# Flamingo-style gated cross attention with routed experts, one core: queries from column-major input and centred weights, the root moved to maxima and exponentials, attention order rewritten

## The reference

```python
x = x + tanh(g_xattn[0]) * xattn(layernorm(x), ctx, Wq, Wkv, null_kv, Wout, ln_scale, ln_bias)
x = x + tanh(g_ffn[0]) * ffn(layernorm(x), ...)      # 32 routed experts, top 8, and a shared one

# xattn
q = split_heads(x @ Wq) * DH ** -0.5
k, v = split_heads(context @ Wkv)                     # null_kv is put in front
attn = softmax(q @ k.T)                               # over 78 columns
out = (attn @ v) @ Wout
out = (out - mean(out)) * rsqrt(var(out) + 1e-6) * ln_scale + ln_bias
```

## Time and profile before

| | us |
|---|---|
| three runs | 2053.12, 2056.40, 2056.99 |
| median | 2056.4 |
| the profiled execution | 2052.15 |
| its span in the trace | 2050.1 |

### The profile page before, as it was taken

The page is one execution under the profiler, slowest core; times in us unless marked ns, Lnnn a source line. Parts: engine busy times, 40 slices in busy tenths (PEclk is TensorE's granted clock), DMA queues, the critical chain, the costliest instruction groups (busy, mean ns, idle before and its releaser), DMA issues.

```text
span 2050.1 us, 43651 instructions
## 1 busy us (share of the span) xinstructions
PE 1947.4 (95%) x14658; PEld 1735.4 (85%) x14658; DVE 1623.5 (79%) x3801; ACT 1377.7 (67%) x3988; POOL 1156.9 (56%) x1254
## 2 busy tenths in 40 slices
PE   7999799999999999999977899999999999999995
PEld 7998689999999999899866788888888888888884
DVE  5544248888888888888867666679999999999996
ACT  2100078888888888888853477777777777777761
POOL 0000103777777777777776000047777777777775
PEclk9999899999999999999978999999999999999997
DMA  8543388877777777777768999999999999999998
GB/s 268 170 143 132 108 307 307 293 253 246 252 250 255 254 247 246 248 255 252 249 229 295 373 285 288 286 327 402 403 393 397 390 398 393 391 397 396 387 363 285
DMA packets 319571, 605.45 MB, mean 295 GB/s; under 512 B 87510, under 2 KB 191671, under 8 KB 319351
## 3 DMA queue, kind: packets, MB, share of 16 engines
q1 hardware_dynamic: 270198, 468.39, 65.7%
q0 software_dynamic: 49152, 134.28, 18.0%
HBM read 305.00 MB, written 297.53 MB: 294 GB/s over the span
## 4 chain that ended last, share of the span: by engine, by line
PE 50%; DMA 17%; DVE 13%; issue 3%; ACT 3%; SPq 2%; DVEq 0%; ACTq 0%
DMA w_raw<-in_experts 15%; PE ring L140 6%; PE sim L1262 6%; PE ring L1326 6%; PE ring L1309 6%; PE ring L141 6%; PE ring L142 6%; DVE parts L1805 4%; PE xps L1902 2%; DVE up_ps L1856 2%; DVE hid_l L1862 2%; DVE w_l L1779 2%; PE gate_ps L140 1%; DVE wq_l L1767 1%; PE gate_ps L141 1%
## 5 line engine op out<-in xcount | busy, mean ns | idle before, releaser
L1696 POOL DMA_INDIRECT parts<-results_dram,kept_index x512 | 516.5, 1009 | 387.2 <-DMA results_dram<-y 219.4
L789 POOL DMA_INDIRECT pages_dram<-rows,kept_index x512 | 537.6, 1050 | 156.2 <-issue 150.0
L847 ACT ACTIVATE exps<-sim,minus_max 128x78 f32<-128x78 f32 x1024 | 317.3, 342 | 23.4 <-DVE minus_max L964 22.6
L1717 ACT ACTIVATE w_h<-w_raw 128x768 fp32r<-128x768 f32 x159 | 134.1, 843 | 157.9 <-DMA w_raw<-in_experts 157.9
L847 ACT ACTIVATION_READ_ACCUMULATOR exps<-sim,minus_max 128x1 f32 x1024 | 229.1, 224 | 0.0
L1805 DVE SCALAR_TENSOR_TENSOR parts<-parts,kept_weight 128x256 f32<-128x256 f32 x448 | 214.0, 478 | 1.3 <-DMA parts<-dense_dram 0.2
L1902 PE MATMUL xps<-ident,xin 128*128 128x128 f32 x1272 | 167.2, 275 | 20.2 <-DVE wq_l L1767 11.5
L1779 DVE TENSOR_TENSOR w_l<-w_raw,w_h 128x768 fp32r<-128x768 f32 x159 | 151.7, 954 | 43.2 <-ACT w_h L1717 42.9
L140 PE MATMUL yps<-w_h,hid_h 128*128 128x256 f32 x636 | 179.5, 282 | 1.4 <-DVE hid_l L1862 1.3
L142 PE MATMUL yps<-w_l,hid_h 128*128 128x256 f32 x636 | 178.4, 281 | 0.0
L141 PE MATMUL yps<-w_h,hid_l 128*128 128x256 f32 x636 | 178.1, 280 | 0.0
(11 more groups left out here) (239 smaller groups left out, 5930.8 us busy)
## 6 DMA issues: line engine op xcount, KB each, us to landing
xin<-pages_dram SPq DMA_DIRECT2D x159, 512.0 KB, 10.5
results_dram<-y SPq DMA_DIRECT2D x159, 512.0 KB, 9.6
w_raw<-in_experts SPq DMA_DIRECT2D x159, 385.0 KB, 9.4
pages_dram<-blank SPq DMA_DIRECT2D x108, 512.0 KB, 4.2
pages_dram<-blank SPq DMA_DIRECT2D x12, 1536.0 KB, 7.0
keys_dram<-keys SPq DMA_DIRECT2D x16, 616.0 KB, 4.3
kT<-keys_dram SPq DMA_DIRECT2D x32, 308.0 KB
v<-values_dram SPq DMA_DIRECT2D x32, 308.0 KB
```

Of the source, the lines that this page charges most:

```text
L789: pool.indirect_dma_start(dram["pages"], bass.IndirectOffsetOnAxis(ap=kept_index[:, at:at + 1].bitcast(U32), axis=0), buffer(batch)[:, k / ...
L847: last = act.activation(exps[u % 2][:, h, :], scores(u)[:, h % 2, h // 2, :], ACT.Exp, bias=minus_max[u][:, h:h + 1], accum_out=row_sum[u] ...
L1696: pool.indirect_dma_start(parts[slot(batch, t)][:, k, :], None, done, bass.IndirectOffsetOnAxis(ap=kept_index[:, at:at + 1].bitcast(U32), ...
```

## The change

- **Queries.** The mean of a row is taken out by centring the columns of Wq instead of the row of x: in the context stage PE multiplies a constant matrix (1/8 by 1/256) with Wq into two free PSUM banks (four products of 512 columns), and DVE subtracts that from Wq/8 in place (four passes of 128x512) before the split. x comes a second time as an input laid out by columns (`in_x_cols`), which is loaded straight into two buffers in turn and split into high and low from SBUF. `apply_x`, the transposes of X and its place in the ring are gone.
- **The root.** The queries lack the factor rstd of their token. DVE multiplies the negated maxima of a unit by it (`scale_maximum`, 128x8, after `maximum`, with a semaphore between), and the exponential takes it as its scale column.
- **Order.** RING, BANK, COPIED and the steps of PE, ACT, DVE, SP and GpSimd are written anew: T1 stands before L and similarity 3, PV0 before the Qs, Q0 to Q2 together, T2b after T3; one scatter moves from between the roots to behind the second; on DVE both parts of `normalise` 0 and 1 come earlier and `weigh` later.

```diff
-RING = ["Oa", "X", "N2", "Ob", "T0a", "T0b", "L", "Q0", "T1a", "Q1", "T1b", "R", "Q2", "PV0a", "PV0b", "T2a", "T2b", "T3a",
-        "T3b", "Q3", "PV1a", "PV1b"]
+RING = ["Oa", "N2", "Ob", "T0a", "T0b", "T1a", "T1b", "L", "PV0a", "PV0b", "Q0", "Q1", "Q2", "T2a", "R", "T3a", "T3b",
+        "T2b", "Q3", "PV1a", "PV1b"]
+BANK = {"Oa": 3, "N2": 2, "Ob": 3, "T0a": 0, "T0b": 1, "T1a": 2, "T1b": 0, "L": 1, "PV0a": 2, "PV0b": 0, "Q0": 1, "Q1": 3,
+        "Q2": 2, "T2a": 1, "R": 3, "T3a": 0, "T3b": 2, "T2b": 1, "Q3": 3, "PV1a": 0, "PV1b": 3}
+COPIED = ["N2", "T0a", "T0b", "X", "T1b", "T1a", "PV0a", "PV0b", "Q0", "Q1", "Q2", "T2a", "T3a", "T2b", "T3b", "Q3", "PV1a",
...
 # context stage, DVE
+            for i in QUERY:
+                dve.wait_ge(averaged, 2)
+                for h in range(INNER // 512):
+                    cols = slice(h * 512, (h + 1) * 512)
+                    last = dve.scalar_tensor_tensor(out=staged(i)[:, cols], in0=staged(i)[:, cols], scalar=SCALE, in1=mean_bank(h)[:, :],
+                                                    op0=ALU.mult, op1=ALU.subtract)
+                last.then_inc(centred, 1)
 # context stage, PE, after the second group's products
+                    for h in range(INNER // 512):
+                        pe.wait_ge(lo, at(CRING, PRODUCTS[len(PRODUCTS) - CBANK + h], g))
+                        for i in QUERY:
+                            pe.wait_ge(w_loaded[i % STAGES], 16 * (i // STAGES + 1))
+                            last = pe.matmul(mean_bank(h)[:, :], column_means[:, :], staged(i)[:, h * 512:(h + 1) * 512],
+                                             start=i == QUERY[0], stop=i == QUERY[-1])
 # attention, SP
-                sp.wait_ge(applied[0], b + 2)
-                sp.dma_start(x_in[:, :, :], x_tiles[b + 2]).then_inc(x_loaded, 16)
+                if b >= 0:
+                    sp.wait_ge(ring_lo, nth(SPLIT, "X", b - 1))
+                load_x(b + 2)
 # GpSimd
-                scatter(b, range(2, 10))
+                scatter(b, range(2, 9))
 # ACT
                 last = act.activation(exps[u % 2][:, h, :], scores(u)[:, h % 2, h // 2, :], ACT.Exp,
-                                      bias=minus_max[u][:, h:h + 1], accum_out=row_sum[u][:, h:h + 1])
+                                      bias=minus_max[u][:, h:h + 1], scale=norm["rstd"][:, b * TT + u % 2:b * TT + u % 2 + 1],
+                                      accum_out=row_sum[u][:, h:h + 1])
-            high("Q0", b)
-            high("T1a", b)
+            high("PV0a", b)
             if here:
                 exp(3, b, 0, PAIRS // 2)
-            high("Q1", b)
-            high("T1b", b)
+            high("PV0b", b)
             if here:
                 exp(3, b, PAIRS // 2, PAIRS)
+            high("Q0", b)
+            high("Q1", b)
             high("Q2", b)
...
 # DVE
-                              ALU.max, negate=True).then_inc(max_done, 1)
+                              ALU.max, negate=True).then_inc(max_made, 1)
+        def scale_maximum(u, b):
+            dve.wait_ge(max_made, UNITS * b + u + 1)
+            dve.tensor_scalar(minus_max[u][:, :], minus_max[u][:, :], norm["rstd"][:, b * TT + u % 2:b * TT + u % 2 + 1], None,
+                              ALU.mult).then_inc(max_done, 1)
 # PE
-            if name == "X":
-                pe.wait_ge(applied[0], b + 2)
-                for c in range(DC):
-                    for t in range(TT):
-                        last = pe.transpose(ps[:, c * N + t * P:c * N + (t + 1) * P], xn[:, t, c * P:(c + 1) * P], ident[:, :])
-                pe.wait_ge(ring_hi, nth(COPIED, ("T1b", "T3a")[half], b))
+                pe.wait_ge(ring_hi, nth(COPIED, ("T1a", "T3b")[half], b))
```

More of the change, by code:

```diff
@@ L214, in context_phase @@
               for j in range(0, 2 * INNER, COLS)]
-    pieces += [(dram["Wq"][c * P:(c + 1) * P, :], [w[:, c, :] for w in wq], SCALE) for c in range(DC)]
+    pieces += [(dram["Wq"][c * P:(c + 1) * P, :], [w[:, c, :] for w in wq], 1.0) for c in range(DC)]
     of_piece = PIECE // D
@@ L566, in attention_phase @@
     grown = sb("grown", [P, ROUTED])
-    x_in = sb("x_in", [P, TT, D])
-    xn = sb("xn", [P, TT, D])
+    x_cols = [sb(f"x_cols{i}", [P, DC, N]) for i in range(2)]
     xnT = [sb(f"xnT_{s}", [P, DC, N], F32R) for s in "hl"]
@@ L583, in attention_phase @@
     gate_ready, rows_ready = sem("gate_ready"), sem("rows_ready")
-    x_loaded, res_loaded = sem("x_loaded"), sem("res_loaded")
+    x_loaded, res_loaded = [sem(f"x_loaded{i}") for i in range(2)], sem("res_loaded")
     keys_loaded = sem("keys_loaded")
@@ L810, in step @@
             if scatters:
-                scatter(b, range(10, 16))
+                scatter(b, range(9, 16))
             if b == B:
@@ L876, in apply_rows @@
             last.then_inc(applied[2], 1)
[L878 to L881, removed]
-                act.wait_ge(norm["ready"], 1)
-            for t in range(TT):
-                at = batch * TT + t
-                last = act.activation(xn[:, t, :], x_in[:, t, :] if batch else rows[0][:, t, 0:D], ACT.Identity,
-                                      bias=norm["shift"][:, at:at + 1], scale=norm["rstd"][:, at:at + 1])
-            last.then_inc(applied[0], 1)
         def step(b, par, h):
@@ L940, in step @@
                 next(dense)
+            high("PV1b", b)
             if 1 <= b <= B:
@@ L1159, in step @@
                 sum_weights(b - 4)
+            if here:
+                scale_maximum(1, b)
             if b >= 3:
@@ L1169, in step @@
                 next(dense)
-            if b >= 3:
-                match(b - 3)
-            if b >= 3:
-                scale_weights(b - 3)
-            if b >= -1:
-                low("X", b)
-            if 1 <= b <= B:
-                add_bias(b, par, h)
+            if here:
+                normalise(1, b)
             if 1 <= b <= B:
@@ L1194, in step @@
                 next(dense)
+            if here:
+                maximum(3, b)
+            if here:
+                scale_maximum(3, b)
             if routes and b < B:
                 route("top", b, par, h)
-            if here:
-                maximum(3, b)
             if 1 <= b <= B:
@@ L1202, in step @@
                 route("mask", b, par, h)
+            if b >= -1:
+                low("PV0a", b)
+            if here:
+                normalise(2, b)
+            if b >= -1:
+                low("PV0b", b)
+            if here:
+                normalise(3, b)
+            if 1 <= b <= B:
+                residual(b, par)
             if b == B:
@@ L1206, in step @@
                 route("placed", b, par, h)
-            if here:
-                normalise(2, b)
-            if 1 <= b <= B:
-                residual(b, par)
-            if here:
-                normalise(3, b)
-            if b >= -1:
-                low("PV0a", b)
-            if b >= -1:
-                low("PV0b", b)
             if 1 <= b <= B:
@@ L1376, in step @@
                 similarity(2, b)
-                similarity(3, b)
+            output("T1a", b, par, h)
+            output("T1b", b, par, h)
             output("L", b, par, h)
@@ L1383, in step @@
                 next(dense)
+            if here:
+                similarity(3, b)
+            output("PV0a", b, par, h)
+            output("PV0b", b, par, h)
             output("Q0", b, par, h)
-            output("T1a", b, par, h)
             output("Q1", b, par, h)
-            output("T1b", b, par, h)
+            output("Q2", b, par, h)
+            output("T2a", b, par, h)
             output("R", b, par, h)
@@ L1391, in step @@
                 next(dense)
-            output("Q2", b, par, h)
-            output("PV0a", b, par, h)
-            output("PV0b", b, par, h)
-            output("T2a", b, par, h)
-            output("T2b", b, par, h)
             output("T3a", b, par, h)
             output("T3b", b, par, h)
+            output("T2b", b, par, h)
             output("Q3", b, par, h)
```

80 lines of the change are left out of this document (52 added, 28 removed).

## The result

| | before | after |
|---|---|---|
| median, us | 2056.69 | 2107.16 |
| lowest to highest | 2053.12 to 2057.45 | 2104.74 to 2108.06 |
| profiled execution | 2052.15 | 2104.74 |
| its span | 2050.1 | 2103.0 |

The ratio of after to before is 1.0248, with a 95% interval of 1.0233 to 1.0263: the change makes the kernel 50.5 us slower. The forecast was 2105, by ScalarE's loop.

The account below looks back on a forecast made before the run. PE bounds the kernel before; the change was to make a loop through ScalarE the bound. 29 x (26.35 - 24.77) = 45.8, + 3 + 1.9 + 0 = +50.7 us, giving a median of 2105 us, range 2050 to 2135.

Parts of the forecast that it names:

- ScalarE's loop: Attention iteration set by ACT's lengthened exponentials: column costs 0.065 to 0.12 us per head, 2077 to 2128 us; chance 0.67.
- The price of the scale column: ACT's exponentials: a second column operand adds 0.095 us each, so eight heads take 3.16 instead of 2.40 us.
- (b): Rival: column hides behind the accumulator's reading, PE stays the bound at 24.33 us per iteration, 2045 us; chance 0.17.
- (c): Rival: column partly hidden or DVE and ACT meet better; iterations 24.8 to 25.4, 2056 to 2079 us; chance 0.12.
- What leaves PE: PE in attention: X's transposes go, 0.44 us per iteration; nothing taken for joining Q0 to Q2; own work becomes 24.33.
- The loop: Attention, similarity 0 to similarity 0 through ACT, DVE and PE: 26.35 us, of which exponentials 12.64 and 13.7 not overlapping.
- The gap from unit 1 to unit 2: Between these units' exponentials DVE's path of 3.71 us decides over PE and ACT's 3.41; first suspect if the loop missed.
- the turn for PE's work: Length of a unit's exponentials at which the bound turns between the loop and PE's work: 2.63 us.
- ACT's sum: ACT's total work per iteration gains 3.0 and loses 1.0 us and still fits: 22.7 of 24.3 us.
- PE's idle time: Late in the iteration, between Q2's last product at 19.6 and T3a at 21.61: about 2 us of PE idle.
- Rival (d): Idle time before T3a drops PE's clock; half-speed T, Q3 and PV1 add up to 4.7 us an iteration, 2240; chance 0.04.
- The rest of the sum: Outside the steady loop: context stage +1.9 us, attention start 0, iterations 0, 1 and 31 1 us each; whole sum +50.7.

Follow-up runs that it names:

- e1: The changed kernel with the exponentials' scale column left out (constant 1.0), all instructions and waits kept: 2043.28 us, ratio 0.994.
- v2: The arithmetic of v1 (root multiplied into x, no scale column) with instructions in the order of the kernel before: 2047.56 us, ratio 0.9954.
- e5: The changed kernel with DVE's maximum of unit 2 and its scaling moved ahead of Ob's statistics and the bias pass: 2097.40 us, ratio 1.0191.
- e3: The kernel before with each exponential taking its scale from a column of ones, same values and order: 2100.17 us, ratio 1.021.
- e4: The changed kernel with the scale column only on the exponentials of units 2 and 3: 2074.95 us, ratio 1.0085.
- e2: The changed kernel without DVE's four scalings of the maxima, scale column kept: 2093.43 us, ratio 1.018.
- v1: The changed kernel with the root multiplied into column-major x by one DVE pass, without scale column or scaled maxima: 2046.88 us, again 2045.83.
- e6: The changed kernel with the scale column kept but the bias column left out of the exponentials: 2044.36 us, ratio 0.9945.

## Why the prediction was right, point by point

**The price of the scale column.** Taken: 0.095 us, wholly in the distance. Measured: 0.444 - 0.348 = 0.096 in the mean record, and eight heads in 3.16, as laid out. That was the step on which the sign hung, and the earlier trace rows were enough for it: an Identity of another width with both columns, against a plain copy. Rivals (b) and (c) needed the column under 0.065. The runs also show that (b)'s time was right for its case: e1 is 2043.28 us with 24.40 per iteration, where (b) said 2045 and 24.33.

**What leaves PE.** Taken were 0.44 us for the transposes of x and nothing for the joined Qs. The first is right, the second was mis-sized. PE of before, the first product of Ob behind the two sets of transposes of the earlier trace rows, and PE of v2, the transposes of N2 and that product:

```profile
609.66 0.37 PE L140 MATMUL ring<-wo_h,outT_h 128*128 128x256 f32 x1
```

```profile
608.78 0.60 PE L1397 MATMUL ring<-ident,rows 128*128 128x128 f32 x4
609.14 0.37 PE L140 MATMUL ring<-wo_h,outT_h 128*128 128x256 f32 x1
```

With x and N2 the transposes take 609.66 - 608.87 = 0.79 in before, with N2 alone 0.36 in v2: 0.43 less. The three Qs take 4.58 apart in before (616.31 to 617.80, 618.16 to 619.67, 620.22 to 621.80) and 4.33 joined in e1 (617.22 to 621.55): 0.25 less. Yet v2's iteration of 24.58 is only 0.19 under 24.77, and e1's 24.40 only 0.37. So some 0.25 to 0.3 comes back in small pieces. In the iterations looked at, Oa takes 0.09 longer in v2 and in e1, PV0 starts 0.12 later behind Q2 in v2, and in e1 the stretch of T0, T1 and similarities 2 and 3 takes 0.19 longer. Why is open. It did not touch the forecast, in which PE was not the bound.

**The loop.** From similarity 0, as predicted and as measured:

| | predicted | measured |
|---|---|---|
| exponentials of unit 0 start | 2.50 | 2.53 |
| unit 1 starts | 6.15 | 6.17 |
| unit 2 starts | 13.02 | 13.03 |
| last exponential done | 20.32 | 20.29 |
| T3a starts | 21.61 | 21.71 |
| Q3 starts | 24.47 - 1.58 = 22.89 | 22.94 |
| next similarity 0 | 26.35 | 26.40 to 26.43 |

The gap from unit 1 to unit 2, named as the first thing to look at, is 3.71 by the rows as it was by the sum. One detail was read otherwise: the trace puts PE's idle time before T2a down to ACT's eviction of Q0, and T3a follows R with no gap. Both releases are near each other: T2a and R need 0.55 (as in e1, where T3a follows T2a by that), which would be 621.79; the probabilities of unit 3 are done at 620.97 + 0.81 = 621.78, and T3a starts at 621.93, 0.15 behind them. So the probabilities come last there, as forecast, and an earlier eviction of Q0 alone would give next to nothing; this was not tried. Two figures of the prediction are slips that nothing rests on: the turn for PE's work is at (24.33 - 13.71) / 4 = 2.66, not 2.63, and ACT's sum is 43.70 / 50 x 24.77 + 2 = 23.6, not 22.7; measured is 44.73 / 50 x 26.43 = 23.6.

**PE's idle time.** "About 2 us" from the end of Q2 to T3a: the last product of Q2 starts at 619.85, T3a at 621.93, with T2a and R between, so that 1.11 before T2a is idle.

**The clock.** Rival (d) did not come: 1.00 in every stretch of 100 us from 300 to 1076, with PE idle 1.6 us of 26.4.

**The rest of the sum**, in the profiled executions. From the spans, 52.9 us are to be found; 50.7 had been summed.

| | predicted | measured |
|---|---|---|
| up to similarity 0 of iteration 0 | +1.9 | +0.8 |
| iterations 0 and 1 | +2 | +2.0 |
| 29 iterations | +45.8 | +48.1 |
| iteration 31 and the experts | +1 | +2.0 |

The second and third rows of the table come from 258.01, 309.71 and 1076.04 in after (the first is below) against 306.88 and 1025.12 before and a first similarity at 257.20. The steady part is short by 2.3, which is 0.08 per iteration, the sum of small differences in the table above. The start was sized 1.1 too high, and its parts were not what I said. The last row is within what this stretch does by itself: from similarity 0 of iteration 31 to the end it takes 1020.9 to 1029.2 us in the other traces and 1040.4 in e5, with the same code for the experts. The steady part, which carries the sum, is confirmed to 2.3 of 48.1; that the whole sum lies within 2 us of the measured one is partly luck, as 2.3 and 1.0 too little stand against 1.1 too much and the noise of that stretch.

```profile
248.61 0.58 PE L140 MATMUL ring<-xnT_h,wq_h 128*128 128x256 f32 x1 [11.53 <-DVE xnT_l L1149]
...
258.01 2.01 PE L1301 MATMUL sim<-kT,qT 64*128 64x78 f32 x32 [0.75 <-ACT qT L899]
```

(PE of after, start of attention.) The context stage's last product starts 2.6 us later than before (236.68 against 234.06), not 1.9; the first Q starts at 248.61, 1.4 later than the 247.18 of the earlier trace rows; and 0.8 is left at similarity 0. Two things give back: x is used 3.0 us after its load is issued (244.11 to 247.13), not 4.4; and in before PE waits 0.74 among the first queries (at 253.38) for the eviction of Q0, which stands behind the normalising of the next x on ACT, a wait that after doesn't have.

**What failed** was in the expectations, not the forecast: e3 by 8 us and e4 by 14. In both I moved one length in a loop that I had laid out for another order or another length, and did not ask again what comes last at each joint. In e4 that was PE's N2, in e3 DVE's low part of PV0a for a part of it. In e2 the same slip, the other path between units 1 and 2, was small. The forecast was spared this since its loop had been laid out instruction by instruction for the order that runs.

## What to carry to other kernels

An activation that runs a thousand times is priced by its operands too: before a factor goes into a scale column beside a bias column, take the price of such an activation from a row of the trace (here 0.1 us each for 1024 of them, 64 us in all) and ask whether the factor can go in elsewhere on an engine with room, as in v1. An engine at 67% busy is not free if its work alternates with another's: four exponentials that overlap none of the 13.7 us between them made the loop, and it passed PE's own 24.4 us while no engine was full. When a loop over engines decides, lay it out anew for each variant, since the wait that is last changes with every length that is moved.

## What was not expected of the hardware

- The recorded duration of an exponential drifts while the distance does not. In after the records grow from 0.42 (602.75, unit 0) to 0.45 (606.39, unit 1), but eight take 3.16 us in the one (to 605.91) and 3.15 in the other (to 609.54). The distance is the cost in the queue.
- A second column on an activation with the accumulator's reading costs in full, 0.39 instead of 0.30 us from one to the next, although a reading that overlaps the next exponential might have covered it; the first column is the same as scale or as bias, 346 and 348 ns (e6, e1).
- The granted clock of PE in iteration 0 differs between kernels that differ little: in the window 275 to 280 it is 0.50 in v1 and 0.91 in v2, which differ in order alone, and 0.67 in e1 and 1.00 in e6, which have one order and differ in an operand. The iteration at the low clock is 3.2 us longer (v1 against v2), as much as the better order earns in 30 iterations.
